# A LayerNorm, attention and mixture-of-experts block on one core: the transposed scores cut into 64 keys, v weighted in 64x32 tiles

## What is computed

```python
xn = _layernorm(x)
q, k, v = split(xn @ w_in.T + b_in)            # 16 heads of 8
scores = einsum('bhqd,bhkd->bhqk', q / sqrt(8), k) + causal_bias
out = einsum('bhqk,bhkd->bhqd', softmax(scores), v) @ w_out.T + b_out
combine = top-2 of softmax(xn @ gate_w.T) over 8 experts, times 2.5
g = silu(einsum('td,edf->etf', xn, w_gate)) * einsum('td,edf->etf', xn, w_up)
y = einsum('te,etd->td', combine, einsum('etf,efd->etd', g, w_down))
return x + out + y + _swiglu_mlp(xn, sw_gate, sw_up, sw_down)
```

## Time and profile before

| | |
|---|---|
| time, median of 3 runs | 576.67 us (576.14 to 577.02) |
| profiled execution | 575.52 us, span 573.8 us |
| TensorE busy | 522.2 us (91%) |
| VectorE busy | 452.5 us (79%) |
| ScalarE busy | 344.8 us (60%) |
| GpSimd busy | 322.3 us (56%) |
| batch to batch in the loop | 66.7 us (209.84 to 276.56) |

### The profile page before, as it was taken

One profiled execution on the slowest core, in us unless ns is written; L12 is line 12 of the kernel. 1 busy time (PEld: TensorE's weight loads), 2 busy tenths in 40 slices (PEclk: granted clock), 3 DMA queues, 4 the chain that ended last, 5 costly groups with the idle time before them and its releaser, 6 DMA issues.

```text
span 573.8 us, 13133 instructions
## 1 busy us (share of the span) xinstructions
PE 522.2 (91%) x4536; PEld 295.5 (51%) x4536; DVE 452.5 (79%) x852; ACT 344.8 (60%) x463; POOL 322.3 (56%) x345
## 2 busy tenths in 40 slices
PE   2679999989999999999999999999999999999985
PEld 1345633656346752576436662466525764366522
DVE  5989798897869968797868968699687978589604
ACT  6422597355963479434983469634794349734693
POOL 2036743775447835479255864478355782558552
PEclk9899999999999999999999999999999999999999
DMA  8984037500475006900268004740069003580001
GB/s 269 267 221 114 12 125 206 132 2 9 146 198 138 2 11 194 261 22 0 104 181 200 0 9 153 220 104 0 22 184 261 18 0 119 164 207 1 10 1 37
DMA packets 45405, 61.99 MB, mean 108 GB/s; under 512 B 4960, under 2 KB 28992, under 8 KB 45376
## 3 DMA queue, kind: packets, MB, share of 16 engines
q1 hardware_dynamic: 42668, 58.37, 36.2%
q10 hardware_dynamic: 2708, 3.24, 1.9%
HBM read 45.21 MB, written 15.34 MB: 106 GB/s over the span
## 4 chain that ended last, share of the span: by engine, by line
PE 60%; DVE 13%; ACT 11%; issue 8%; POOL 5%; DMA 2%; ACTq 1%; POOLq 0%; DVEq 0%
PE banks L673 10%; ACT probs L934 8%; PE banks L537 7%; PE banks L538 6%; PE banks L539 6%; PE banks L573 6%; PE banks L553 6%; PE banks L646 6%; DVE neg_max L1253 5%; PE banks L555 3%; PE banks L554 3%; POOL hid_lo L1024 2%; DVE probs L1229 2%; POOL probs L1044 1%; POOL probs L1016 1%
## 5 line engine op out<-in xcount | busy, mean ns | idle before, releaser
L1253 DVE TENSOR_REDUCE neg_max<-banks 128x2 f32<-128x1024 f32 (+7 forms) x240 | 178.3, 794 | 17.2 <-PE banks L564 16.8
L934 ACT ACTIVATE probs<-banks 128x1024 f32<-128x1024 f32 x160 | 155.4, 1031 | 11.4 <-PE banks L646 9.2
L1044 POOL TENSOR_SCALAR_AFFINE_SELECT probs<-probs 128x512 f32<-128x512 f32 x128 | 90.8, 732 | 124.0 <-ACT probs L934 124.0
L1016 POOL TENSOR_TENSOR probs<-probs,cb 128x512 f32<-128x512 f32 x88 | 113.2, 1286 | 81.4 <-ACT probs L871 80.9
L871 ACT ACTIVATE probs<-banks 128x512 f32<-128x512 f32 (+1 forms) x112 | 67.0, 598 | 134.2 <-PE banks L539 133.9
L1024 POOL TENSOR_TENSOR hid_lo<-probs,hid_hi 128x512 fp32r<-128x512 f32 x85 | 109.6, 1290 | 36.6 <-ACT hid_hi L878 36.3
L1229 DVE TENSOR_TENSOR probs<-probs,banks 128x512 f32<-128x512 f32 (+1 forms) x112 | 76.4, 683 | 35.8 <-POOL probs L1016 27.7
L537 PE MATMUL banks<-x_hi,w_hi 128*128 128x512 f32 (+1 forms) x224 | 95.0, 424 | 4.4 <-DVE probs L1229 4.4
L673 PE MATMUL banks<-probs,v_op 128*32 128x512 f32 (+3 forms) x1024 | 95.2, 444 | 3.7 <-POOL probs L1044 3.5
L538 PE MATMUL banks<-x_lo,w_hi 128*128 128x512 f32 (+1 forms) x224 | 89.0, 398 | 0.0
L539 PE MATMUL banks<-x_hi,w_lo 128*128 128x512 f32 (+1 forms) x224 | 88.8, 396 | 0.0
(11 more groups left out here) (136 smaller groups left out, 552.3 us busy)
## 6 DMA issues: line engine op xcount, KB each, us to landing
cb<-c_dram SPq DMA_DIRECT2D x31, 256.0 KB, 3.9
q_op<-q_dram SPq DMA_DIRECT2D x15, 512.0 KB, 6.8
k_op<-k_dram SPq DMA_DIRECT2D x15, 512.0 KB, 8.2
cb<-c_dram SPq DMA_DIRECT2D x16, 224.0 KB, 4.3
q_dram<-q_parts SPq DMA_DIRECT2D x8, 384.0 KB, 2.5
k_dram<-k_parts SPq DMA_DIRECT2D x8, 384.0 KB, 2.5
cb<-c_dram SPq DMA_DIRECT2D x16, 192.0 KB, 4.2
cb<-c_dram SPq DMA_DIRECT2D x15, 160.0 KB, 4.3
```

The source lines that it names most:

```text
L934: nc.scalar.activation(probs[:, g % 2, 2 * u:2 * u + 2, :], ring[:, at:at + 2, :], ACT.Exp).then_inc(exp_done, 1)
L1016: nc.gpsimd.tensor_tensor(sg[k % 3][:, :], sg[k % 3][:, :], cb[:, tiles_of(b)[k], :], ALU.mult).then_inc(weighted, 1)
L1044: return nc.gpsimd.affine_select(out=view, in_=view, compare_op=ALU.is_ge, fill=0.0, base=0, pattern=[[0, 4], [1, P]], channel_multiplier=-1)
L1253: return nc.vector.tensor_reduce(out, in_, AX.X, ALU.max, negate=True)
```

## The change

The transposed scores are cut into blocks of 64 keys. A unit (`keys_of`) now holds the four heads of one quad: tile column c takes one pair of heads, bank a one head of each, and the partitions 64c to 64c + 63 hold 64 keys. Key block w of 64 has 512 - 64w queries, and block 8 - w fills the rest of the 512 columns; the block 4 of two quads shares a unit. That makes 9 units for two quads, 18 a batch, for 20 before. Each unit is made by four or eight matmuls in 64x64 tiles and four more that add the mask to the diagonal blocks. GpSimd's selects are gone, with the semaphore `masked`.

`weigh_v` takes steps of two units: eight tiles of 64x32 (two halves of the partitions, four heads each), which write to the two banks of `nat`. A step w has the blocks w and 8 - w, so 512 columns, and the fifth 256: ten steps a batch. A step is issued once three more units of scores have been (`WEIGH_BEHIND`). Both banks are complete only after the last step, so both copies, transpositions and divisions of o now stand in the expert stage of the next batch, and in the tail for the last batch. `transpose_on` moves behind the gate matmuls of k = 3, ScalarE's copy of it with it. The last two steps stand behind the first gate matmuls of the next batch.

v and the logits are projected in 16 matmuls of 64 tokens and half of the heads, in two tile columns; v, its bias and the output weights get a matching layout, loaded by two more DMAs for the weights of v, one more for the bias and four more for the output weights. `probs` becomes a ring of 12 units of 1024 columns (`home_of`), `att` shares the memory of `o_norm`. The core of the diff:

```diff
+ST_ALL = NAT_ALL
+WEIGHINGS = OWN_UNITS + 1
+PV_ALL = GROUPS // 2 * WEIGHINGS
+VG = E // 2 + NE
+PROBS = 12
+LEFT = 10
...
+WEIGH_BEHIND = 3
+TURN_COMB_AT = 13
...
+def keys_of(n):
+
+    t, v = divmod(n, TWO_QUADS)
+    if v == 2 * OWN_UNITS:
+        return [(2 * t, JQ // 2, 0), (2 * t + 1, JQ // 2, S // 2)]
+    g, w = 2 * t + v % 2, v // 2
+    return [(g, w, 0)] + [(g, JQ - w, S - HALF * w)] * int(w > 0)
+
+
+def home_of(n):
+
+    t, v = divmod(n, TWO_QUADS)
+    return (LEFT * t + v) % PROBS
+
+
+def weighing_of(t, w):
+
+    n = TWO_QUADS * t + 2 * w
+    if w == OWN_UNITS:
+        return [(JQ // 2, (n, n), (0, S // 2))]
+    return [(w, (n, n + 1), (0, 0))] + [(JQ - w, (n, n + 1), (S - HALF * w,) * 2)] * int(w > 0)
+
+
+def last_unit_of(t, w):
+    return TWO_QUADS * t + min(2 * w + 1, 2 * OWN_UNITS)
...
-        att = sb("att", [P, QT, E])
-
...
-        last_o = [banks[:, n, 0:S // 2] for n in (0, 1)]
+        o_banks = [nat[:, 0, :], nat[:, 1, :]]
+        last_o = [banks[:, n, :] for n in (0, 1)]
         last_on = [banks[:, n, 0:S // 2] for n in (2, 3)]
...
-            sp.dma_start(wvg_sb[:, 0:E], wvT).then_inc(vl_weights, 16)
-            sp.dma_start(wvg_sb[:, E:E + NE], gateT).then_inc(vl_weights, 16)
+            for c in range(2):
+                sp.dma_start(wvg_sb[:, c, 0:E // 2].rearrange("p (g n) -> p g n", g=GROUPS),
+                             wvT.rearrange("e (g c n) -> c e g n", g=GROUPS, c=2)[c]).then_inc(vl_weights, 16)
+                sp.dma_start(wvg_sb[:, c, E // 2:VG], gateT).then_inc(vl_weights, 16)
             sp.dma_start(bqk[:, :], b_qk).then_inc(qk_weights, 16)
...
+                sp.dma_start(bv_bc[half(c), :].rearrange("p (g n) -> p g n", g=GROUPS),
+                             b_v.rearrange("(g c n) -> c g n", g=GROUPS, c=2)[c].partition_broadcast(HALF)
+                             ).then_inc(bv_loaded, 16)
             sp.dma_start(lower_sb[:, :, :], lower.partition_broadcast(P)).then_inc(consts_loaded, 16)
             for dst, src in ((mask_f[0:HALF, :], causal[0:HALF, 0:HALF]), (mask_f[HALF:P, :], causal[0:HALF, 0:HALF]),
...
+                for jk in range(JQ):
+                    for c in range(2):
+                        at = jk ^ c
+                        n = VG if at % 2 == 0 else E // 2
+                        mm = pe.matmul(vl[half(c), at // 4, at % 4, 0:n], xnT[:, jk * HALF:(jk + 1) * HALF],
+                                       wvg_sb[:, c, 0:n], start=True, stop=True, tile_position=(0, HALF * c),
+                                       skip_group_check=True)
                 mm.then_inc(vl_ready, 1)
...
                 if k == 0 and i is not None:
-                    pe.wait_ge(o_normed, OUTS * i + 1)
...
@@ -634,52 +674,49 @@
                     pe.wait_ge(hid_done, NT * i + NT)
                 elif n >= 2:
                     pe.wait_ge(exp_done, ST_ALL * i + n - 1)
-                for a in range(2):
...
+                apart(pe, pe_passed)
+                blocks = keys_of(n)
+                for m, (g, jk, at) in enumerate(blocks):
+                    for c in range(2):
+                        for a in range(2):
+                            pe.matmul(ring[half(c), 2 * ((n + 1) % 2) + a, at:at + S - HALF * jk],
+                                      k_op[half(a), 2 * g + c, HALF * jk:HALF * (jk + 1)],
+                                      q_op[half(a), 2 * g + c, HALF * jk:S], start=(m == 0), stop=False,
+                                      tile_position=(HALF * a, HALF * c), skip_group_check=True)
+                for c in range(2):
+                    for a in range(2):
+                        mm = mask_scores_t(ring[half(c), 2 * ((n + 1) % 2) + a, :], a, c, blocks)
                 mm.then_inc(st_ready, 1)
 
...
+            def mask_scores_t(bank, a, c, blocks):
+
+                second = blocks[-1][2] // HALF
+                diagonal = bank.rearrange("p (k n) -> p k n", n=HALF)[:, 0:second + 1:max(second, 1), :]
+                return pe.matmul(diagonal, mask_half[half(a), :],
+                                 ident_half[half(a), :].unsqueeze(1).to_broadcast([HALF, len(blocks), HALF]),
+                                 start=False, stop=True, tile_position=(HALF * a, HALF * c), skip_group_check=True)
+
+            def weigh_v(i, t, w, front):
+
+                pe.wait_ge(exp_done, ST_ALL * i + last_unit_of(t, w) + 1)
+                if t == 0 and w == 0:
+                    pe.wait_ge(v_placed, i + 1)
+                    if front:
+                        pe.wait_ge(q_done, i + 2)
+                        pe.wait_ge(k_done, i + 2)
+                apart(pe, pe_passed)
+                for jk, units, at in weighing_of(t, w):
+                    for c in range(2):
+                        for j in range(4):
+                            x, a = j // 2, j % 2
+                            mm = pe.matmul(nat[32 * j:32 * j + 32, c, HALF * jk:S], v_op[half(c), jk ^ c, t, j, :],
+                                           probs[half(c), 2 * home_of(units[x]) + a, at[x]:at[x] + S - HALF * jk],
+                                           start=(t == 0 and jk == 0), stop=(t == 1 and jk == JQ // 2),
+                                           tile_position=(HALF * c, 32 * j), skip_group_check=True)
+                mm.then_inc(pv_done, 1)
 
...
                     if k == 2:
+                        transpose_o(i, 0)
                         transpose_o(i, 1)
+                    if k == 3:
+                        transpose_on(i)
                     ahead = int(k < EARLY)
...
                         down(b, k - 2, i)
-                    if k == 2:
-                        transpose_on(i)
...
-                    for u in range(UNITS):
...
+                steps = [(t, w) for t in range(GROUPS // 2) for w in range(WEIGHINGS)]
+                m = 0
+                for n in range(2, ST_ALL):
+                    scores_t(i, n)
+                    if n == 2 and front:
+                        project_q(i + 1)
+                    if n == 3:
+                        transpose_y(i)
+                    if n == TURN_COMB_AT and front:
+                        transpose_comb(i + 1)
+                    if n >= WEIGH_BEHIND + last_unit_of(*steps[m]):
+                        weigh_v(i, *steps[m], front)
+                        m += 1
+                if front:
+                    pair(i + 1, i, 0)
+                    gate_up(i + 1, 0)
+                for step in steps[m:]:
+                    weigh_v(i, *step, front)
+                if front:
+                    pair(i + 1, i, 1)
+                    gate_up(i + 1, 1)
 
             pe.wait_ge(ident_loaded, 16)
             transpose_x(0)
-            pe.wait_ge(vl_weights, 16 * 2)
+            pe.wait_ge(vl_weights, 16 * 4)
             project_v_and_logits(0, vl_first)
             pe.wait_ge(qk_weights, 16 * 2)
             project_q(0)
...
+                    if k == 3 and i is not None:
+                        act.wait_ge(onT_ready, i + 1)
+                        nc.scalar.activation(o_normT[:, :], nat[:, 0, :], ACT.Copy).then_inc(onT_done, 1)
...
                         square_root(1)
-                    if k == 2 and i is not None:
-                        act.wait_ge(onT_ready, i + 1)
...
-                            if (g, u) == (0, 1):
-                                exp_router(i + 1)
-                            if (g, u) == (0, 2):
-                                take_q(i + 1)
+                before(act, pv_done, PV_ALL * i)
+                for n in range(ST_ALL):
+                    t, v = divmod(n, TWO_QUADS)
+                    act.wait_ge(st_ready, ST_ALL * i + n + 1)
+                    if home_of(n) in (LEFT - 3, LEFT - 2):
+
+                        act.wait_ge(hid_lo_done, NT * i + NT - 2 + home_of(n) - (LEFT - 3))
+                    if t == 1 and v >= 2 and v % 2 == 0:
+
+                        act.wait_ge(pv_done, PV_ALL * i + v // 2)
+                    at = 2 * ((n + 1) % 2)
+                    nc.scalar.activation(probs[:, 2 * home_of(n):2 * home_of(n) + 2, :], ring[:, at:at + 2, :], ACT.Exp
+                                         ).then_inc(exp_done, 1)
...
-                    buf = probs[:, g % 2, :, :]
-                    first = ST_ALL * i + UNITS * g
-                    pool.wait_ge(exp_done, first + 2)
-                    mask(buf[:, 0:4, 0:P]).then_inc(masked, 1)
-                    pool.wait_ge(exp_done, first + 4)
-                    mask(buf[:, 4:8, 0:P]).then_inc(masked, 1)
-                    mask(buf[:, 4:8, 3 * P:4 * P]).then_inc(masked, 1)
-                    pool.wait_ge(exp_done, first + 5)
-                    mask(buf[:, 8:10, :].rearrange("p b (j n) -> p (b j) n", j=2)[:, :, 0:P]
-                         ).then_inc(masked, 1)
-
...
             with pool.Fori(1, NB - 2) as i:
-                attend(i)
                 experts(i + 1, i)
...
+                        normalise_o(i, 0)
```

(5 more changed lines are left out.)

198 lines of the change are left out of this document (63 added, 135 removed).

## The result

The changed kernel takes 582.6 us (median, 581.69 to 590.78) where the kernel before takes 576.6: a ratio of 1.0099 with the 95% interval 1.0079 to 1.0119, so 1% slower. The forecast was 571.4 in a range from 564 to 581. The profiled execution took 582.21 us, its span is 580.4.

A forecast was written before the change was run, and what follows sets the result against it. ScalarE's exponentials bound the attention half, TensorE and VectorE the expert half. Per batch -2.8 + 2.0 + 0.15 = -0.65, seven times -4.6, start +0.8, end -1.5: -5.3 us, to 571.4; range 564 to 581.

The forecast's parts named there:

- Weighing step: Attention half, TensorE: eight 64x32 tiles overlap fully, 1.03 us per 512-column step; a batch's weighing changes by -1.4 us.
- Projection of v: Directly ahead of the transposed scores, TensorE: 1.15 us instead of 1.02, +0.15 a batch, bounds 0 and +0.7.
- Attention half: From first transposed scores to G0, paced by ScalarE's exponentials: 2.8 us shorter a batch (2.3 to 3.5).
- G0: Start of the next batch's first gate matmul, 233.01 before; divides attention half from expert half; forecast 230.2.
- Expert half: After G0, shared by TensorE and VectorE: moved work adds 2.0 us a batch (1.3 to 2.4); pair 4 10.7 after G0.
- The end: Last batch, no expert half: weighing ends about 2.4 us earlier, more copies and turns cost +0.9; together -1.5 us.
- Front end: TensorE's queue: about 56 loads and matmuls per 0.98 us, 17 ns each, cost nothing; margin under two.
- the start: Before the first batch: two more loads on SP's queue delay the q and k weights, +0.8 us (0 to +1.5).
- B: Rival: without the exponentials' slips and pair 4's added idleness, a batch gains 2.1 to 2.2 us; 561, half 566; chance 0.12.
- E: Rival: fewer exponentials free nothing because TensorE is as late as ScalarE; counted in C, no chance of its own.
- C: Rival: eight weighing tiles cost more than four; 576 at 1.16 us a step, 580 at 1.25; chance 0.23.
- D: Rival: small costs take the gain, v's projection +0.7 and exponential slips 1.2; 579.5, half of them 575; chance 0.15.

The follow-up runs named there:

- the loops that fit: Changed kernel without the mask matmuls of its transposed scores, 569.3 us, and the same with GpSimd masking the probabilities, 570.2 us; neither fetches instructions in its loop.
- the one with GpSimd's masks: Changed kernel with the transposed scores' mask put on the probabilities by GpSimd instead of TensorE, full output: 570.2 us, ratio 0.990 to the kernel before.
- a loop of 1751: Changed kernel with transposed scores masked by two matmuls over all 128 rows instead of four in 64x64 tiles: 589.9 us, ratio 1.019 to the kernel before.
- 1679 at one of two places: Changed kernel without transposed-score masks, with 188 idle instructions ahead of TensorE's program: 600.2 us in one execution; without those instructions 569.3.
- all six rows: Table of loops of 1494, 1679, 1751, 1679, 1823 and 1878 instructions: the first two fetched 0 blocks, the third 9 once, the others 9 a pass.
- the variant with one transfer: Changed kernel, loop kept, with the weights of v and gate in one transfer and the bias in one: 582.1 us, ratio 1.011 to the kernel before.
- the program with one transfer: Changed kernel with one transfer for the weights of v and gate, and TensorE's loop written out straight: 577.0 us, ratio 0.999 to the kernel before.

## Why the prediction was wrong

*Right.* The terms of TensorE's own work held. Weighing step 1.03 us (220.55 to 221.58), as taken for full overlap of eight 64x32 tiles. Here the Trainium skill (TensorE: Matmul & The Clock Gate, Measured speedup vs the span model) had spoken for an estimated 1.15; the trace doesn't agree for these tiles. Projection of v 1.12 (212.03 to 213.15) for 1.15. Attention half: scores to G0 22.06 us, 20.16 without the two stalls of "issue", for 23.17 before: -3.0 for -2.8. Expert half: pair 4 at G0 + 10.64 with 1.38 idle, for 10.7 and 1.3; from G0 to the next scores, the projection of v included, 45.6 us for 43.55, +2.05 for +2.15. The undisturbed batch is 1.0 shorter for 0.65, and in the loops that fit 1.3 to 1.4. The end: -1.8 for -1.5.

*The step that failed* is "Front end": "about 56 loads and matmuls per 0.98 us, 17 ns each ... So this costs nothing, but the margin is under two." It asked only how fast instructions can be issued, and never how many there are in a pass of the loop and where they come from. That can be read from the trace of before: 1238 instructions in a pass, none fetched between 220 and 480 us. The change adds 585. At 1823 all of them are fetched in every pass; each jump stalls TensorE by 1.6 to 2.0 us and the dense weighings behind it by 0.35 to 0.66; the nine stalls of 0.3 us and more that nothing releases add to 10.0 us, and the four long batches are 10.2 us longer than four of 65.75. Taken off the 582.2 of that execution, this leaves an estimated 572, beside the forecast of 571.4. No run has the kernel as changed, with its tiled masks, in a loop that stays; the nearest is the one with GpSimd's masks, 570.2. That the forecast is so near both is partly luck, since two sizes offset each other: in that run a batch is 1.3 us shorter for 0.65, and the start costs more than the 0.8 taken. None of the rivals B to E was this; C and D reached the right side for reasons that the rows refute, since neither the tiles nor the small costs were dearer.

The Trainium skill has the rule (Runtime: NRT & Kernel Launch, Instruction fetch mechanics): TensorE holds 128 KiB, 2048 instructions, as a FIFO of 16 KiB blocks, and a taken jump to something outside the current window of two pages waits for a transfer. The transfers of 16384 bytes and the 3.7 us agree. The window of two pages doesn't: a loop of 1751 ran three passes without a transfer. Nor does its 2048 serve as a limit for a loop: 1823 didn't stay, nor did 1679 at one of two places. Eight blocks, of which one is read beyond the loop's end, fit all six rows but the one of 1751, which fetched nine blocks once and then none; this reading is worked out, not shown.

*A term mis-sized* is the start: +0.8 taken, 4.7 measured in the profiled executions and 2.9 in the mean of all. Two further transfers were counted on SP's queue (bq_scaled 2.0 us later, for 0.9 at 0.45 each; all four for v and gate took 0.56 to 0.88, where the two of before took 0.43). The other 2.7 come behind it: pair 0 waits for k until 37.03 (before 34.81), and TensorE, busy for 6.9 us from 30 to 40 (before 7.4), had a clock of 0.73 from 40 to 50 us, where before and the variant with one transfer have 1.00. But since this variant won almost nothing at the end, the start isn't what made the prediction wrong.

## What to carry to other kernels

Before splitting matmuls, count the instructions of a pass of the loop on the engine concerned and look for instruction transfers in the steady state: as long as there are none, more instructions of the right length are cheap; past a limit (here between 1500 and 1800 on TensorE, depending on the loop's place) each pass pays for all of them. Then it is worth giving a cheap operation to an idle engine, as with the masks here, even where TensorE does it in 0.16 us. If the loop can't be made to stay, choose for its jump a place where matmuls are queued and no large transfer is under way, and don't count on the engine's own waiting to hide it.

## What the runs showed of the hardware

- From a jump to the next instruction: 0.2 us where the pass fetches nothing; 3.3 to 3.9 us where it does (0.9 to 1.6 until the block moves, 0.9 to 1.4 in transfer, 1.3 to 1.5 behind it; once 4.4); 5.0 to 9.0 us at eight jumps behind transfers that keep the DMA engines busy.
- A straight program isn't free of it: with 1823 instructions in 66 us single stalls of 0.5 to 3.6 us come at places that change (the longest, 3.60, at 430.5 us of the program with one transfer), and the time varies by 1.3% from run to run; with 1238 in 66.7 us nothing is lost.
- Whether a loop stays depends on its place: 188 instructions ahead of it turned one that stayed into one that didn't, and its passes went from 65.3 to between 67.5 and 68.6 us.
- Masks over all 128 rows between matmuls in 64x64 tiles cost 0.32 us a unit of two blocks (0.56 less the 0.24 of its scores), where four tiled ones cost 0.16.
- Eight tiles of 64x32 with four-byte data overlap fully: 1.03 us for 512 columns, as four of 128x32 take 1.00.
